# Mixture-of-experts kernel: rows stored in token order, gathered by the experts, instead of scattered by the router

## The chip, the cores and the metric

One core of one Trainium2 chip runs the whole program. The metric is device time in microseconds (us), the median of the runs. Engines: TensorE (PE; its weight loads are PEld), VectorE (DVE), ScalarE (ACT), GpSimd (POOL) and SyncE (SP), whose queue issues most transfers.

## What is computed

x has 4 x 1024 tokens of 256 values. Two layers follow each other, each a cross attention and a feed-forward block. The change lies in the last block, a mixture of 8 experts with 2 of them for each token. Cut to what matters:

```python
logits = layernorm(x) @ Wr + br                  # 4096 x 8
top2 values and indices -> weights w (softmax over the two)
for each token t, for each of its two experts e:
    h = relu(layernorm(x)[t] @ W1[e] + b1[e])    # 256 -> 1024
    out[t] += w * (h @ W2[e] + b2[e])            # 1024 -> 256, on top of the residual x[t]
```

## The kernel before

The 32 tiles of 128 tokens pass through two stages, `route` and `experts`, each a block of its own: all engines leave a block together, and the next one's work begins after that.

**route.** ScalarE normalises a tile into a ring `pay` (`norm`, L1885; 4 buffers of 4 tiles), TensorE transposes it and multiplies it by Wr, ScalarE copies the transposed tile (`copy`, L1891). Every four tiles make a chunk: VectorE picks the two experts of each token (`choose`), ScalarE takes the exponential (`ratio`, L1900), and VectorE (`place`) writes expert, weights and token number beside the row and computes, from a running count per expert (TensorE products with a triangle and with ones, `rank`), the place of each row in a table sorted by expert, `xs` in HBM. GpSimd then scatters each tile's rows twice, once for each expert, with indirect DMAs (L1828, 64 of them, 130 KB each). `norm` waits until the scatters that used its buffer have landed. Between these, 16 halves of W2 come through a ring of four (`load_half`, L1781, SP's queue), ScalarE makes their f16 high part (`high`, L1895) and VectorE their low part (`low`, L1971); the halves of a chunk are split after `place` of that chunk, and half q is loaded once half q-4 is split. The list HIGHS puts two halves into each of chunks 1 to 5 and three into chunks 6 and 7. At the end VectorE computes which expert each of the 32 whole tiles (256 rows) and of the 7 half tiles (128 rows) belongs to, and SP writes rows of padding behind each expert's last row.

**experts.** 36 tiles: 32 of 256 rows with one expert each, then 4 "mixed" ones made of the 7 half tiles. Each engine runs its own list of steps k; in step k

- TensorE turns tile k+2 (`turn_x`, L2184, waits for its rows), multiplies tile k+1 by W1 (`up`) and tile k by W2 (`down`), in this order;
- ScalarE makes the high part of the turned tile k+2 (`high_x`), then the relu of tile k+1;
- VectorE takes the low part of the turned tile k+2 (`rest_x`, L2279), then weighs the result of tile k-1 (`weigh`: yb L2300, yo L2308), then handles the token numbers and splits the relu's output (L2288, L2290);
- GpSimd adds the weighed rows of a tile into the output in HBM, 128 rows at a time, with an accumulating indirect DMA (`add`, L2333), each only after the one before it has landed;
- SP loads the rows of tile k+3 (260 KB, plain DMA, two buffers) once its buffer is free.

A step's signals are semaphores that count tiles; an engine's instructions run in the order of its list.

Of the kernel before, what the change touches and what calls it, by code (L numbers as in the profile page):

```python
# [19 lines left out]
F32 = mybir.dt.float32  # L20
# [1690 lines left out]
def route(nc, w, router, b1T, eid, x_res, mv, rstd, nmr, ident, w2, ssq, sums, unscale, xs, acc, table):  # L1711
# [3 lines left out]
    NB = 4  # L1715
    NK = NT // TK
    NS = 4
    HIGHS = ((),) + 5 * ((1, 3),) + 2 * ((0, 1, 3),)
    with Scope(nc, "rt") as s:
# [16 lines left out]
        posf = s.sb("posf", [P, TK, 2])  # L1736
        pos = [s.sb(f"pos{j}", [P, TK, 2], U32) for j in range(NB)]
        tok = s.sb("tok", [P, NT], U32)
        base = s.sb("base", [P, E])
# [6 lines left out]
        ntf, nti, jump = s.sb("ntf", [P, 2, E]), s.sb("nti", [P, 2, E], I32), s.sb("jump", [P, 2, E])  # L1746
        cum, want, give, left = (s.sb(n, [P, 2, E]) for n in ("cum", "want", "give", "left"))
        whole, lone, spare, twice = s.sb("whole", [P, E + 1]), s.sb("lone", [P, E]), s.sb("spare", [P, 1]), s.sb("twice", [P, 1])
        tid = s.sb("tid", [P, ND + NH])
        ge = s.sb("ge", [P, ND + NH, E])  # L1750
        tf = s.sb("tf", [P, 2, ND + NH])
# [4 lines left out]
        (cst, xn_r, t_r, xt_r, sc_mm, sc_r, c, e_r, d_r, b1_t, b1_c, ind_r, rank_mm, cnt_r, padded,  # L1756
         meta_r) = (s.sem(n) for n in (
            "cst", "xn_r", "t_r", "xt_r", "sc_mm", "sc_r", "c", "e_r", "d_r", "b1_t", "b1_c", "ind_r",
            "rank_mm", "cnt_r", "padded", "meta_r"))
        sent = [s.sem(f"sent{j}") for j in range(NB * TK)]  # L1760
# [14 lines left out]
        @block.sync  # L1775
        def _(sp):
            def load_half(q):
                src = w["L1_ffn_W2"]
                rows = src.shape[1] // 2
                need(sp, wlo_r, q - NS + 1)  # L1780
                sp.dma_start(stage[q % NS][:, :].rearrange("p (t n) -> p t n", n=src.shape[2]),  # L1781
                             src[q // 2, (q % 2) * rows:(q % 2 + 1) * rows, :].rearrange("(t p) n -> p t n", p=P)
                             ).then_inc(half_in[q % NS], 16)

            for q in range(NS):
                load_half(q)
            router["copy"](sp, E - 1)
            for q in range(NS, 2 * E):
                load_half(q)
            sp.wait_ge(cst, CONSTS)  # L1790
            for q in range(TR // P):
                sp.dma_start(xs[E * CAP + q * P:E * CAP + (q + 1) * P, :], pad[:, :]).then_inc(padded, 16)
            sp.wait_ge(cnt_r, 1)
            for e in range(E):
                n = nc.sync.value_load(cnt[0:1, e:e + 1], min_val=0, max_val=T)
                for q in range(TR // P):
                    sp.dma_start(xs[bass.ds(n + (e * CAP + q * P), P), :], pad[:, :]).then_inc(padded, 16)
            sp.wait_ge(padded, 16 * (E + 1) * (TR // P))
            sp.wait_ge(acc_in, 16 * E)

        @block.gpsimd
        def _(pool):
# [3 lines left out]
            g.iota(base[:, :], pattern=[[CAP, E]], base=0, channel_multiplier=0,  # L1806
# [5 lines left out]
            g.memset(whole[:, E:E + 1], 0.0).then_inc(cst, 1)  # L1812
# [5 lines left out]
            pool.wait_ge(cst, 10)  # L1818
            g.affine_select(out=tri[:, :], in_=tri[:, :], compare_op=ALU.is_gt, fill=0.0, base=0,
                            pattern=[[1, P]], channel_multiplier=-1).then_inc(cst, 1)  # L1820
            g.memset(run[:, :], 0.0).then_inc(cst, 1)

            last_row = g.to_reg(E * CAP - 1)
            for t in range(NT):
                c, i = divmod(t, TK)
                pool.wait_ge(meta_r, c + 1)
                for k in range(2):
                    g.indirect_dma_start(out=xs[:, :], out_offset=bass.IndirectOffsetOnAxis(ap=pos[c % NB][:, i, k:k + 1], axis=0),  # L1828
                                         in_=pay[c % NB][:, i, :], in_offset=None, bounds_check=last_row,
                                         oob_is_err=True).then_inc(sent[t % (NB * TK)], 16)  # L1830
            for j in range(NB * TK):
                pool.wait_ge(sent[j], 32 * len(range(j, NT, NB * TK)))

        @block.tensor
        def _(pe):
# [21 lines left out]
            def rank(c):  # L1857
                pe.wait_ge(ind_r, c + 1)
                if c == 0:
                    pe.wait_ge(b1_c, 1)  # L1860
                    pe.wait_ge(bmr_r, 1)
                nc.tensor.matmul(ps_c[0][:, 0:TK * E], tri[:, :], ind[:, :, :], start=True, stop=True).then_inc(rank_mm, 1)
                nc.tensor.matmul(ps_c[1][:, 0:TK * E], ones[:, :], ind[:, :, :], start=True, stop=True).then_inc(rank_mm, 1)

            for t in range(NT):
# [7 lines left out]
                if t % TK == 2 and t > TK:  # L1873
                    rank(t // TK - 1)
            score(NT - 1)
            rank(NK - 1)

        @block.scalar
        def _(act):
            def norm(t):  # L1880
                c, i = divmod(t, TK)
                need(act, sent[t % (NB * TK)], 32 * (c // NB))
# [14 lines left out]

            def ratio(c):
                act.wait_ge(d_r, c + 1)
                nc.scalar.activation(wt[:, 1, :], wt[:, 0, :], ACT.Exp).then_inc(e_r, 1)  # L1900
# [4 lines left out]
            for t in range(NT):  # L1905
# [10 lines left out]
            ratio(NK - 1)  # L1916

        @block.vector
        def _(dve):
# [62 lines left out]
            def choose(c):  # L1982
# [11 lines left out]
                link_on(last)  # L1994
                link_on(v.tensor_copy(idf[:, :, :], idx[:, :, 0:2]))
                if c == 0:
                    dve.wait_ge(cst, CONSTS)
                for n in range(2):
                    last = v.tensor_tensor(oh[:, n, :, :], idf[:, :, n].unsqueeze(2).to_broadcast([P, TK, E]),
                                           eid[:, :].unsqueeze(1).to_broadcast([P, TK, E]), ALU.is_equal)  # L2000
                link_on(last)
                v.tensor_tensor(ind[:, :, :], oh[:, 0, :, :], oh[:, 1, :, :], ALU.add).then_inc(ind_r, 1)

            def place(c):

                out = pay[c % NB]
                for i in range(TK):
                    need(dve, sent[c % NB * TK + i], 32 * (c // NB))
# [3 lines left out]
                link_on(v.tensor_tensor(out[:, :, D + 2], wt[:, 1, :], wt[:, 2, :], ALU.mult))  # L2012
                v.tensor_tensor(out[:, :, D + 1], wt[:, 2, :], out[:, :, D + 2], ALU.subtract)
                v.tensor_copy(out[:, :, D], idf[:, :, 0])
                v.tensor_copy(out[:, :, D + 3].bitcast(U32), tok[:, TK * c:TK * c + TK])

                dve.wait_ge(rank_mm, 2 * (c + 1))
                link_on(v.tensor_copy(tot[:, :, :], ps_c[1][:, 0:TK * E].rearrange("p (t e) -> p t e", e=E)))
                for e in range(E):
                    last = v.tensor_tensor_scan(incl[:, :, e], ones[:, 0:TK], tot[:, :, e], run[:, e:e + 1],  # L2020
                                                ALU.mult, ALU.add)
                link_on(last)
                v.tensor_copy(run[:, :], incl[:, TK - 1, :])

                link_on(v.tensor_tensor(tot[:, :, :], incl[:, :, :], tot[:, :, :], ALU.subtract))
                link_on(v.tensor_tensor(tot[:, :, :], ps_c[0][:, 0:TK * E].rearrange("p (t e) -> p t e", e=E), tot[:, :, :],
                                        ALU.add))
                link_on(v.tensor_tensor(tot[:, :, :], tot[:, :, :], base[:, :].unsqueeze(1).to_broadcast([P, TK, E]), ALU.add))
                for n in range(2):
                    last = v.tensor_tensor(oh[:, n, :, :], oh[:, n, :, :], tot[:, :, :], ALU.mult)  # L2030
                link_on(last)
                for n in range(2):
                    last = v.tensor_reduce(posf[:, :, n], oh[:, n, :, :], AX.X, ALU.add)
                link_on(last)
                v.tensor_copy(pos[c % NB][:, :, :], posf[:, :, :]).then_inc(meta_r, 1)
# [13 lines left out]
            then(v.tensor_copy(cnt[:, :], run[:, :]))  # L2049
            dve.sem_inc(cnt_r, 1)  # L2050

            def per_tile(x, k):
                return x.unsqueeze(1).to_broadcast([P, (ND, NH)[k], E])
# [15 lines left out]
            v.tensor_tensor(whole[:, 0:E], ntf[:, 0, :], lone[:, :], ALU.add)  # L2069
            then(v.scalar_tensor_tensor(out=left[:, 0, :], in0=left[:, 0, :], scalar=2.0, in1=left[:, 1, :],  # L2070
                                        op0=ALU.mult, op1=ALU.add))
            v.tensor_tensor_scan(cum[:, 0, :], ones[:, 0:E], whole[:, 0:E], 0.0, ALU.mult, ALU.add)
            v.tensor_scalar(jump[:, 0, :], whole[:, 0:E], -1.0, float(CAP // TR), ALU.mult, ALU.add)
            v.tensor_tensor(lone[:, :], whole[:, 1:E + 1], whole[:, 0:E], ALU.subtract)
            v.tensor_scalar(twice[:, :], whole[:, 0:1], 2.0, None, ALU.mult)
# [376 lines left out]
```

## Time and profile before

| | us |
|---|---|
| median of 3 runs (1394.09 to 1397.82) | 1396.09 |
| the profiled execution | 1395.44 |
| its span in the profile | 1393.7 |
| all before the routing stage (0 to 856) | 856 |
| routing stage up to the last scores (856 to 941) | 85 |
| from there to the first transpose of the experts (941 to 969) | 28 |
| expert stage (969 to the end) | 425 |

The profile's times count from the start of the span. A row of a timeline gives start, duration, engine, line, operation, output<-input, shape, count, and in brackets how long the engine had been idle before it and what ended that. "PEclk" is the granted share of TensorE's clock (1.00 is 2.4 GHz, 0.50 is 1.2 GHz). "Landing" is the time from a transfer's issue until its semaphore says that it is done.

### The profile page before, as it was taken

The numbers are of one execution on the slowest core, as the hardware profiler recorded it, in microseconds if no ns is written. First come the engines' busy times: TensorE is split into PE (matmuls) and PEld (weight loads), VectorE is DVE, ScalarE is ACT, GpSimd is POOL, SyncE is SP. The second block draws the span as 40 slices with busy tenths as digits, with TensorE's granted clock in tenths as the row PEclk, the third lists the DMA queues.
The fourth block names the chain that finished last, engine by engine and source line by source line (L and its number), as shares of the span: only waits on it lengthen the run. The fifth ranks groups of instructions, "written<-read, shape, count | busy, mean of one in ns | idle before, by whom it ended". The sixth has DMA issues, their size and how long they took to land. (4 is left out here: it accounts for less than half of the span.)

```text
span 1393.7 us, 28305 instructions
## 1 busy us (share of the span) xinstructions
PE 1207.5 (87%) x8633; PEld 922.0 (66%) x8634; DVE 1023.8 (73%) x2058; ACT 802.4 (58%) x1214; POOL 519.4 (37%) x423
## 2 busy tenths in 40 slices
PE   8799999959987767998999997631999999999995
PEld 4457777734432555785777776621889898999874
DVE  5879999887999594786989897944565666656542
ACT  4675656466599697557888886630434344333341
POOL 2077777600000001004888882773123222232222
PEclk9899999989999557999999998555999999999998
DMA  6010000000034873002234323564222323322210
GB/s 232 9 64 1 0 0 0 0 1 0 23 159 178 263 260 131 1 1 66 77 93 125 99 91 125 184 201 153 43 48 46 49 46 47 53 46 45 48 30 7
DMA packets 61448, 106.07 MB, mean 76 GB/s; under 512 B 7488, under 2 KB 48704, under 8 KB 60736
## 3 DMA queue, kind: packets, MB, share of 16 engines
q1 hardware_dynamic: 48080, 88.24, 19.9%
q0 software_dynamic: 13296, 16.92, 6.5%
q8 instruction: 38, 0.62, 0.2%
q14 instruction: 34, 0.28, 0.1%
HBM read 66.96 MB, written 39.10 MB: 76 GB/s over the span
## 5 line engine op out<-in xcount | busy, mean ns | idle before, releaser
L2333 POOL DMA_INDIRECT out<-ex_yo,ex_mt x71 | 114.2, 1608 | 317.2 <-DVE ex_yo L2308 169.0
L2242 ACT ACTIVATE ex_hT<-ex_ps_h,e_b1T,e_unscale 128x256 f32<-128x256 f32 (+1 forms) x312 | 143.9, 545 | 114.5 <-PE ex_ps_h L2199 114.5
L2199 PE MATMUL ex_ps_h<-ex_xT_hi,a_arena 128*128 128x256 f16 (+1 forms) x1248 | 202.7, 266 | 0.6 <-issue 0.5
L604 PE MATMUL at_ps_y<-c_VW,at_pT_hi 128*128 (+1 forms) x1024 | 171.1, 273 | 3.5 <-DVE main_x_res L752 3.5
L946 POOL TENSOR_TENSOR at_sc<-at_sc,at_ri 128x960 f32<-128x960 f32 (+1 forms) x96 | 144.9, 1523 | 56.4 <-DVE at_ri L747 56.0
L2199 PE MATMUL ex_ps_h<-ex_xT_lo,a_arena 128*128 128x256 f16 (+1 forms) x624 | 164.1, 264 | 0.0
L946 POOL TENSOR_TENSOR at_sc<-at_sc,at_mx 128x960 f32<-128x960 f32 (+1 forms) x96 | 134.1, 1411 | 70.3 <-DVE at_mx L724 70.2
L2212 PE MATMUL ex_ps_y<-a_arena,ex_hT_hi 128*128 x568 | 155.7, 274 | 4.8 <-DVE ex_hT_lo L2290 2.7
L582 PE MATMUL at_ps_s<-a_arena,at_xnT_hi 128*128 (+1 forms) x512 | 155.1, 385 | 3.0 <-issue 2.9
L2212 PE MATMUL ex_ps_y<-e_w_lo,ex_hT_hi 128*128 x568 | 155.7, 274 | 0.0
L2212 PE MATMUL ex_ps_y<-a_arena,ex_hT_lo 128*128 x568 | 155.6, 274 | 0.0
L1189 PE MATMUL gm_bank<-f_xq,f_wide 128*128 (+1 forms) x576 | 129.3, 385 | 13.3 <-DVE f_xq L1281 7.0
L604 PE MATMUL at_ps_y<-c_VW,at_pT_lo 128*128 (+1 forms) x512 | 139.6, 273 | 0.0
L2199 PEld LDWEIGHTS ex_ps_h<-ex_xT_hi,a_arena 128*128 x1248 | 121.6, 98 | 18.2 <-issue 1.9
L643 ACT COPY at_sc<-at_ps_s 128x1024 f32<-128x1024 f32 x64 | 64.7, 1010 | 98.5 <-PE at_ps_s L582 98.5
L1189 PEld LDWEIGHTS gm_bank<-f_xq,f_wide 128*128 128x128 f16 x576 | 55.9, 99 | 86.5 <-issue 8.9
L604 PEld LDWEIGHTS at_ps_y<-c_VW,at_pT_hi 128*128 128x128 f16 x1024 | 100.0, 98 | 15.0 <-issue 4.2
L2233 ACT ACTIVATE ex_xT_hi<-ex_ps_t 128x512 f16<-128x512 f32 (+1 forms) x36 | 21.3, 591 | 150.5 <-PE ex_ps_t L2184 150.5
L724 DVE TENSOR_REDUCE at_mx<-at_sc 128x16 f32<-128x960 f32 (+1 forms) x96 | 79.0, 850 | 38.6 <-ACT at_sc L643 38.6
L582 PE MATMUL at_ps_s<-a_arena,at_xnT_lo 128*128 (+1 forms) x256 | 98.2, 384 | 0.0
L2288 DVE CAST ex_hT_hi<-ex_hT 128x1024 f16<-128x1024 f32 (+1 forms) x72 | 52.6, 731 | 56.9 <-ACT ex_hT L2242 56.8
L2279 DVE SCALAR_TENSOR_TENSOR ex_xT_lo<-ex_ps_t,ex_xT_hi 128x512 f16<-128x512 f32 (+1 forms) x36 | 24.6, 684 | 91.1 <-ACT ex_xT_hi L2233 91.1
(352 smaller groups left out, 2778.7 us busy)
## 6 DMA issues: line engine op xcount, KB each, us to landing
at_half<-in_L_ffn_W SPq DMA_DIRECT2D x32, 512.0 KB, 4.1
up_scratch<-gm_stg SPq DMA_DIRECT2D x16, 768.0 KB, 3.2
gm_stg<-up_scratch SPq DMA_DIRECT2D x16, 768.0 KB, 4.3
ex_row<-xs SPq DMA_DIRECT2D x32, 260.0 KB, 3.0
rt_stage<-in_L_ffn_W SPq DMA_DIRECT2D x16, 512.0 KB, 4.8
main_x_res<-in_x SPq DMA_DIRECT2D x8, 512.0 KB, 12.0
out<-main_x_res SPq DMA_DIRECT2D x8, 512.0 KB, 6.4
xs<-rt_pad SPq DMA_DIRECT2D x18, 130.0 KB, 2.4
```

Source lines behind the costliest of these rows:

```text
L582: last = nc.tensor.matmul(ps_s[j][:, c * CH:(c + 1) * CH], a[:, d, :], b[:, d, bass.ds(off + c * CH, CH)], start=(n == 0), stop=(n == 3 * ...
L604: last = nc.tensor.matmul(ps_y[:, 0:D], a[j][:, n, :], b[:, bass.ds(off + n * D, D)], start=(n == 0 and i == 0), stop=(n == NP - 1 and i = ...
L643: nc.scalar.copy(sc[j][:, :, :], ps_s[j % 2][:, :].rearrange("p (h k) -> p h k", h=H)).then_inc(ev_r, 1)
L724: last = nc.vector.tensor_reduce(mx[:, j, :, g], sc[j][:, :, lo:hi], AX.X, ALU.max)
L946: last = nc.gpsimd.tensor_tensor(part, part, what[:, j, :, g].unsqueeze(2).to_broadcast([P, H, hi - lo]), op)
L1189: last = nc.tensor.matmul(ps[:, o, :], a[:, d, o * P:(o + 1) * P], b[:, d, bass.ds(c0, CH)], start=(n == 0), stop=(n == 3 * DT - 1))
L2199: last = nc.tensor.matmul(ps_h[:, n, at], a[:, bass.ds(e * WN + d * HID + n * P, P)], b[:, d, at], start=(m == 0), stop=(m == 3 * DT - 1))
L2212: last = nc.tensor.matmul(ps_y[j][:, q, :], a[:, n, q * P:(q + 1) * P], b[:, bass.ds(e * WN + n * D, D)], start=(n == 0 and m == 0), stop= ...
L2242: last = nc.scalar.activation(hT[:, n, at], ps_h[:, n, at], ACT.Relu, bias=b1T[:, bass.ds(e * HT + n, 1)], scale=unscale[:, 0, bass.ds(e, 1)])
L2279: nc.vector.scalar_tensor_tensor(out=xT_lo[j][:, :, at], in0=ps_t[:, :, at], scalar=XN_SCALE, in1=xT_hi[j][:, :, at], op0=ALU.mult, op1=AL ...
L2288: nc.vector.tensor_copy(hT_hi[j][:, part, at], hT[:, part, at]).then_inc(hhi_r, 1)
L2333: nc.gpsimd.indirect_dma_start(out=acc[:, :], out_offset=bass.IndirectOffsetOnAxis(ap=mt[j][:, q, 1:2].bitcast(U32), axis=0), in_=yo[j][:, ...
```

## The change

- Each normalised row is written once, in token order, with plain DMAs from ScalarE's queue (`send`, one per chunk of 4 tiles, 520 KB), two chunks after its normalisation; the ring `pay` has three buffers instead of four. The 64 scatters and SP's 16 writes of padding behind the experts' rows go; one block of padding rows is written.
- The small sums and copies beside the rows move from VectorE to GpSimd; the ranks of all tiles are computed at once after the last chunk, by two larger products.
- A list `slot` is made in their place: for each of the 71 blocks of 128 rows and each lane, the number of the row in `xs`. VectorE writes 0/1 masks (`spread`, four groups of 16 token columns: 71 x 16, 71 x 16 and 128 x 16 values per partition), ScalarE scales one of them, and 64 products on TensorE add them up.
- In the expert stage GpSimd fetches a block's rows with an indirect DMA through `slot` (two for each tile, four row buffers); SP loads nothing but b2. Of a whole tile both additions are issued without waiting for one another; they wait for those of the tile before. The loops are unrolled by four tiles instead of two.

The core of the diff (renamed indices, sizes and semaphores left out):

```diff
 # route, ScalarE
+            def send(c):
+                act.wait_ge(xn_r, TK * (c + 1))
+                act.wait_ge(pay_r, c + 1)
+                nc.scalar.dma_start(xs[(TK * c + 1) * P:(TK * (c + 1) + 1) * P, :].rearrange("(i p) d -> p i d", p=P),
+                                    pay[c % NB][:, :, :]).then_inc(sent[c % NB], 16)
...
-                need(act, sent[t % (NB * TK)], 32 * (c // NB))
+                need(act, sent[c % NB], 16 * (c // NB))
...
                 if t % TK == 1 and t > TK:
                     ratio(t // TK - 1)
+                if t % TK == 1 and t > 2 * TK:
+                    send(t // TK - 2)
                 if i in HIGHS[c]:
                     high(highs_to(c) + HIGHS[c].index(i))
             ratio(NK - 1)
+            send(NK - 2)
+            send(NK - 1)
+            for g in range(NG):
+                act.wait_ge(spot_r, g + 1)
+                need(act, slot_mm, g - 1)
+                nc.scalar.activation(in_slot[g % 2][:, 1, :, :], is_slot[g % 2], ACT.Copy, scale=lane[:, 0:1]).then_inc(slot_r, 1)
 # route, VectorE, place(c): all but the first two operations go (weights and token numbers to GpSimd)
                 link_on(v.tensor_scalar(wt[:, 0, :], wt[:, 1, :], 1.0, None, ALU.add))
-                link_on(v.reciprocal(wt[:, 2, :], wt[:, 0, :]))
...
+                v.reciprocal(wt[:, 2, :], wt[:, 0, :]).then_inc(inv_r, 1)
 # route, VectorE, after the last chunk (some 20 small operations between, the quotas as before)
+            dve.wait_ge(rank_mm, 1)
+            dve.wait_ge(xn_r, NT)
+            dve.wait_ge(acc_in, 16 * E)
+            then(v.tensor_copy(tot[:, :, :], ps_c[1][:, 0:NT * E].rearrange("p (t e) -> p t e", e=E)))
+            for e in range(E):
+                last = v.tensor_tensor_scan(incl[:, :, e], ones[:, 0:NT], tot[:, :, e], 0.0, ALU.mult, ALU.add)
...
+            def spread(g):
+                mine, t0 = slice(GR * g, GR * g + GR), GR * g % NT
+                need(dve, slot_r, g - 1)
+                need(dve, turn_r, g - 1)
+                v.tensor_tensor(is_slot[g % 2], line[:, 0:SLOTS].unsqueeze(1).to_broadcast([P, GR, SLOTS]),
+                                part_f[:, 1, mine].unsqueeze(2).to_broadcast([P, GR, SLOTS]), ALU.is_equal).then_inc(spot_r, 1)
+                need(dve, slot_mm, g - 1)
+                dve.wait_ge(spot_r, g + 1)
+                v.tensor_tensor(in_slot[g % 2][:, 0, :, :], is_slot[g % 2],
+                                turn_no[:, t0:t0 + GR].unsqueeze(2).to_broadcast([P, GR, SLOTS]), ALU.mult).then_inc(turn_r, 1)
+                v.tensor_tensor(in_lane[:, mine, :], line[:, :].unsqueeze(1).to_broadcast([P, GR, P]),
+                                part_f[:, 0, mine].unsqueeze(2).to_broadcast([P, GR, P]), ALU.is_equal).then_inc(lane_r, 1)
...
             lows(highs_to(NK - 1), highs_to(NK))
+            dve.wait_ge(slot_mm, NG)
+            then(v.tensor_copy(lane_v[:, :], ps_i[:, SLOTS:2 * SLOTS]))
+            v.scalar_tensor_tensor(out=slot[:, :], in0=ps_i[:, 0:SLOTS], scalar=float(P), in1=lane_v[:, :], op0=ALU.mult, op1=ALU.add)
 # experts, GpSimd (RB = 4, Q = 2; SP's load() goes)
+            def fetch(i, q):
+                need(pool, t_r, i - RB + 1)
+                need(pool, meta_r, i - RB + 1)
+                n = 2 * i + q
+                nc.gpsimd.indirect_dma_start(out=row[i % RB][:, q, :], out_offset=None, in_=xs[:, :],
+                                             in_offset=bass.IndirectOffsetOnAxis(ap=slot[:, n:n + 1].bitcast(U32), axis=0),
+                                             bounds_check=last_sent, oob_is_err=True).then_inc(row_in[i % RB], 16)
+            def add(i, q):
                 pool.wait_ge(yo_r, i + 1)
-                for q in range(rows_of(i).stop):
-                    need(pool, added, 16 * (Q * i + q))
+                need(pool, added, 16 * (Q * i + (q if mixed(i) else 0)))
                 pool.sem_inc(begun, 1)
...
+            for i in range(RB):
+                for q in range(Q):
+                    fetch(i, q)
+            for k in range(1, NTL + 1):
+                for q in range(rows_of(k - 1).stop):
+                    add(k - 1, q)
+                if there(k + 3, NTL):
+                    for q in range(rows_of(k + 3).stop):
+                        fetch(k + 3, q)
```

## Rows read from the trace of the kernel before

**Rows 1.** Stretches of the span: busy time of each engine, clock, DMA.
```profile
core 0: us, PE busy (x) PEld busy (x) DVE busy (x) ACT busy (x) POOL busy (x), PEclk, DMA share, GB/s
...
820.00:856.00 36.00, 28.89 (x235) 23.25 (x233) 30.51 (x70) 23.74 (x36) 21.14 (x23) 1.00 0.24 74
...
880.00:890.00 10.00, 6.09 (x28) 5.77 (x28) 9.14 (x59) 5.85 (x12) 7.87 (x8) 0.50 0.66 217
...
1060.00:1100.00 40.00, 40.00 (x369) 35.99 (x367) 25.49 (x43) 17.24 (x35) 11.11 (x7) 1.00 0.31 50
```

**Rows 2.** Timeline of GpSimd in the routing stage, the scatters.
```profile
868.85 1.33 POOL L1828 DMA_INDIRECT xs<-rt_pay,rt_pos  x1 [11.36 <-DVE rt_pos L2035]
...
885.84 1.86 POOL L1828 DMA_INDIRECT xs<-rt_pay,rt_pos  x1 [0.30 <-issue]
...
956.39 0.97 POOL L1828 DMA_INDIRECT xs<-rt_pay,rt_pos  x1 [0.30 <-issue]
```

**Rows 3.** Timeline of ScalarE in the routing stage.
```profile
869.66 0.37 ACT L1891 COPY rt_xt<-rt_ps_t 128x256 f32<-128x256 f32 x1
...
891.16 1.15 ACT L1895 ACTIVATE a_arena<-rt_stage,rt_wsc 128x1024 f16<-128x1024 f32 x1 [2.17 <-DMA rt_stage<-in_L_ffn_W]
...
896.27 0.37 ACT L1891 COPY rt_xt<-rt_ps_t 128x256 f32<-128x256 f32 x1
...
936.44 1.15 ACT L1895 ACTIVATE a_arena<-rt_stage,rt_wsc 128x1024 f16<-128x1024 f32 x1 [10.43 <-DMA rt_stage<-in_L_ffn_W]
```

**Rows 4.** One line, L1781: the halves of W2, issue to landing.
```profile
DMA to landing us min/median/max: 4.2/4.8/7.1
```

**Rows 5.** One line, L1828: the scatters, issue to landing.
```profile
DMA to landing us min/median/max: 2.4/3.1/7.2
```

**Rows 6.** One line, L2333: the additions, issue to landing.
```profile
DMA to landing us min/median/max: 2.7/4.0/6.2
```

**Rows 7.** Timeline, from the last scores to the first expert matmul.
```profile
940.37 0.19 DVE L1985 TENSOR_TENSOR rt_scores<-rt_ps_r,e_brb 128x32 f32<-128x32 f32 x1 [5.80 <-PE rt_ps_r L1853]
...
942.31 0.19 DVE L2002 TENSOR_TENSOR rt_ind<-rt_oh 128x32 f32<-128x32 f32 x1
...
946.87 0.17 DVE L2055 TENSOR_SCALAR rt_nti<-rt_cnt 128x8 int32<-128x8 int32 x1
...
949.79 0.17 DVE L2077 SCALAR_TENSOR_TENSOR rt_jump<-rt_lone,rt_left 128x8 f32<-128x8 f32 x1
...
952.69 3.68 DVE L1971 SCALAR_TENSOR_TENSOR e_w_lo<-rt_stage,rt_wsc,a_arena 128x1024 f16<-128x1024 f32 x3
...
973.30 0.39 PE L2199 MATMUL ex_ps_h<-ex_xT_hi,a_arena 128*128 128x256 f16 x1
```

**Rows 8.** Groups by line and shape, VectorE, routing and expert stages.
```profile
L2020 DVE TENSOR_TENSOR_SCAN rt_incl<-rt_ones,rt_run,rt_tot 128x4 f32<-128x4 f32 x64 | 9.4, 220 | 0.3
...
L2086 DVE TENSOR_TENSOR rt_ge<-rt_ge,rt_jump 128x256 f32<-128x256 f32 x1 | 0.4, 426 | 0.0
...
L2290 DVE TENSOR_TENSOR ex_hT_lo<-ex_hT,ex_hT_hi 128x1024 f16<-128x1024 f32 x70 | 85.8, 1225 | 2.4
```

**Rows 9.** Timeline of the expert stage: transposes of a tile, products, additions.
```profile
991.42 0.60 PE L2184 MATMUL ex_ps_t<-main_ident,ex_row 128*128 128x128 f32 x4
...
1089.67 0.60 PE L2184 MATMUL ex_ps_t<-main_ident,ex_row 128*128 128x128 f32 x4
...
1092.91 0.69 DVE L2308 TENSOR_TENSOR ex_yo<-ex_yb,ex_mt 128x512 f32<-128x512 f32 x1
...
1094.48 1.62 POOL L2333 DMA_INDIRECT out<-ex_yo,ex_mt  x1 [3.96 <-DVE ex_yo L2308]
...
1100.17 1.54 POOL L2333 DMA_INDIRECT out<-ex_yo,ex_mt  x1 [4.07 <-DMA out<-ex_yo,ex_mt]
...
1319.47 0.60 PE L2184 MATMUL ex_ps_t<-main_ident,ex_row 128*128 128x128 f32 x4
...
1333.95 0.60 PE L2184 MATMUL ex_ps_t<-main_ident,ex_row 128*128 128x128 f32 x4
```

More of the change, by code:

```diff
@@ L56 @@
 NTL = ND + NM
+SLOTS = 2 * ND + NH
 EPS = 1e-5
@@ L2014, in place @@
[L2014 to L2030, printed above, removed]
@@ new lines, in _ @@
+            then(v.tensor_tensor(begin[:, 1, :], begin[:, 1, :], begin[:, 0, :], ALU.subtract))
+            then(v.tensor_tensor(incl[:, :, :], incl[:, :, :], begin[:, 1, :].unsqueeze(1).to_broadcast([P, NT, E]), ALU.mult))
+            then(v.tensor_tensor(after[:, :, :], after[:, :, :], incl[:, :, :], ALU.add))
+            for i in range(2):
+                last = v.tensor_tensor(oh[:, i, :, :], oh[:, i, :, :], after[:, :, :], ALU.mult)
+            then(last)
+            then(v.tensor_reduce(spot[:, :], oh[:, :, :, :].rearrange("p n t e -> p (n t) e"), AX.X, ALU.add))
@@ L2099, in experts @@
+            lows(highs_to(NK - 1), highs_to(NK))
+            dve.wait_ge(slot_mm, NG)
+            then(v.tensor_copy(lane_v[:, :], ps_i[:, SLOTS:2 * SLOTS]))
+            v.scalar_tensor_tensor(out=slot[:, :], in0=ps_i[:, 0:SLOTS], scalar=float(P), in1=lane_v[:, :],
+                                   op0=ALU.mult, op1=ALU.add)
+def experts(nc, b2, b1T, eid, x_res, w1, w2, unscale, ident, xs, acc, table, slot):
     Q = TR // P
     with Scope(nc, "ex") as s:
-        row = [s.sb(f"row{j}", [P, Q, ROW]) for j in range(2)]
+        RB = 4
+        row = [x_res[:, E:, :].rearrange("p t d -> p (t d)")[:, j * Q * ROW:(j + 1) * Q * ROW].rearrange("p (q d) -> p q d", q=Q)
+               for j in range(RB)]
@@ L2144, in landed, with in_fours @@
             if not mixed(i):
[L2145 to L2148 removed]
+                return 16 * Q * (i // RB + 1)
+            return 16 * (Q * ND // RB + sum(len(runs(m)) for m in range(ND + i % RB, i + 1, RB)))
+        def in_fours(eng, lead, lag, step):
             for k in range(-lead, 4):
[L2151 to L2156 removed]
+                step(k, k % RB)
+            with eng.Fori(1, ND // RB - 1, 1) as i:
+                for j in range(RB):
+                    step(RB * i + j, j)
+            for k in range(ND - RB, NTL + lag):
+                step(k, k % RB)
         @block.sync
         def _(sp):
[L2160 to L2173 removed]
             sp.dma_start(b2s, b2.unsqueeze(0).to_broadcast([P, E, D])).then_inc(b2_in, 16)
[L2175 removed]
         @block.tensor
@@ L2187, in up @@
             def up(i, j):
-                spans = [(look_up(nc.tensor, 1, n, E - 1), slice(q0 * P, q1 * P)) for n, q0, q1 in runs(i)]
+                spans = [(expert(nc.tensor, n), slice(q0 * P, q1 * P)) for n, q0, q1 in runs(i)]
                 pe.wait_ge(xhi_r, i + 1)
@@ L2204, in down @@
             def down(i, j):
-                spans = [(look_up(nc.tensor, 1, n, E - 1), range(q0, q1)) for n, q0, q1 in runs(i)]
+                spans = [(expert(nc.tensor, n), range(q0, q1)) for n, q0, q1 in runs(i)]
                 pe.wait_ge(hlo_r, 2 * i + 2)
@@ L2235, in relu @@
             def relu(i, j):
-                spans = [(look_up(nc.scalar, 1, n, E - 1), slice(q0 * P, q1 * P)) for n, q0, q1 in runs(i)]
+                spans = [(expert(nc.scalar, n), slice(q0 * P, q1 * P)) for n, q0, q1 in runs(i)]
                 for g in range(2):
@@ L2259, in take_meta @@
                 q = rows_of(i)
-                nc.vector.tensor_copy(meta[j][:, q, :], row[j][:, q, D:ROW]).then_inc(meta_r, 1)
+                nc.vector.tensor_copy(meta[j % 2][:, q, :], row[j][:, q, D:ROW]).then_inc(meta_r, 1)
             def keep_meta(i, j):
-                spans = [(look_up(nc.vector, 1, n, E - 1), slice(q0, q1)) for n, q0, q1 in runs(i)]
+                spans = [(expert(nc.vector, n), slice(q0, q1)) for n, q0, q1 in runs(i)]
                 need(dve, added, 16 * Q * (i - 1))
@@ L2293, in weigh @@
             def weigh(i, j):
-                spans = [(look_up(nc.vector, 1, n, E - 1), slice(q0, q1)) for n, q0, q1 in runs(i)]
+                spans = [(expert(nc.vector, n), slice(q0, q1)) for n, q0, q1 in runs(i)]
                 if isinstance(i, int) and i == 0:
```

255 lines of the change are left out of this document (125 added, 130 removed).

## The prediction

> **What bounds the kernel now.** I read the busy time of the engines by stretches first, then the timeline of each stage that the change touches, then single lines for the landing times.
>
> In the expert stage TensorE is the bound: between 1060 and 1100 it is busy 40.00 of 40 us at full clock [rows 1]. The transposes that open its steps (I call that time X) stand at 991.42 for the turn of tile 3 and at 1319.47 for tile 33, 30 steps of 10.93 us [rows 9]. GpSimd's waits there are long, for the weighed rows and for the addition before, but TensorE waits for none of them.
>
> In the routing stage TensorE does not count (6.09 of 10 us, clock 0.50, which is 1.2 GHz [rows 1]). GpSimd sends 64 scatters from 868.85 on, the last starting at 956.39, one each 1.27 us (0.97 and a gap of 0.30) with few breaks [rows 2]; VectorE waits for them before it may write beside a row. ScalarE waits for halves of W2 that SP can load only after VectorE's split, 10.43 us the longest [rows 3]. So this stage is a chain of scatters and VectorE's chunks, and its end a tail of 32.9 us from the last scores (940.37) to the first expert product (973.30) [rows 7].
>
> **The change, part 1: the routing stage up to the last scores.** The scatters go; with them the pace of 10 us per chunk. What is late next is ScalarE. Without a wait it does two highs and four pairs of norm and copy from 891.16 to 896.64, 5.48 us, so 1.05 for a high and 0.85 for a pair [rows 3]. But with three buffers the norm of the first tile of chunk C+1 waits for the send of chunk C-2, which ScalarE issued only one high and one pair earlier. No row shows a send from this queue. The nearest is a half of W2, about the same size: 4.2 to 7.1 us, median 4.8 [rows 4]; I take 4.8. After the wait come three pairs, a high and the exponential, 3.8 us: 8.6 us a chunk. The first such send can go after the copy that ended at 870.03 [rows 3], so at 870.2; four chunks later 904.6, with the third high of chunk 6 905.7. Then two waits for halves of W2 remain that the change doesn't remove: the half is loaded after `place` and one split (1.9 us), and lands 4.8 us later, 6.7 in all. The first takes us to 912.4, two highs, two pairs and the exponential to 916.4, the second to 923.1. In the kernel before, the high after this same wait started at 936.44 and the last scores were there at 940.37 [rows 3, 7], 3.9 later. So now 927.0 in place of 940.4: 13.4 us earlier. With 4.2 in all six waits it is 17.0, with 7.1 nothing (0.4 later).
>
> The sends' issue on ScalarE I cost inside the 4.8, behind which nothing else waits. The sums moved to GpSimd are hidden: it has nothing else to do in this stage, and `send` of a chunk comes two chunks later; without that cover each would cost ScalarE about 1 us a chunk. The rank products per chunk leave TensorE, which isn't the bound: nothing.
>
> **Part 2: the tail.** From the last scores, all on one chain: `choose` up to the masks 1.9 (940.37 to 942.3 [rows 7]); GpSimd's sum and the first rank product 1.7 (estimate: before, two products of an eighth of the columns and VectorE's sum took 1.4); copy, 8 scans of 32 and differences 3.2 (0.22 for a scan of 4 and 0.43 for 256 elements [rows 8]; a scan between 0.15 and 0.5, I take 0.25); the quotas as before 2.9 (946.87 to 949.79 [rows 7]); twelve operations for the positions 5.1 (five of 256 at 0.43, one of 512, the rest at 0.2 [rows 7, 8]); the masks: 256 elements take 0.43 and 1024 take 1.225 us, so 1.04 ns an element [rows 8], 1.3 for 1136 and 2.3 for 2048, four groups of 4.9, 19.5; the table of tiles 1.3; three lows 3.7 [rows 7]; the list itself 0.5. That makes 39.8. ScalarE's scaling and TensorE's 64 products run under the masks and the lows; without that cover they would add some 4 us. Then leaving the block 0.3, four fetches issued in 5.1 (0.97 and a gap of 0.30, as the scatters [rows 2]), landing 3.1 [rows 5], transposes 1.1: 49.4 in place of 32.9. The tail is 16.5 us longer (13.5 to 19.5 with the scans, the small operations and the landing at their ends). What went from it, the last scatters and the writes of padding, is contained in the 32.9.
>
> Both parts: 16.5 - 13.4 = 3.1 us later, from 3.5 earlier to 20 later.
>
> **Part 3: the expert stage.** "Four tiles ahead" counts buffers. On GpSimd, whose list is in order, the fetch of tile k+3 stands behind the two additions of tile k-1. Their rows are ready only in step k, because VectorE's `weigh` of k-1 stands behind `rest_x` of k+2, which needs the transposes that open step k. And the transposes of tile k+3 open step k+1. So the rows are asked for in one step and needed at the start of the next, and the way round is a loop: transposes, low part, weigh, two additions, two fetches, landing, next transposes. Its length from the rows: transposes at 1089.67, weighed rows at 93.60, first addition issued at 94.48 [rows 9], 4.81 after X. It keeps GpSimd 1.62. The second follows at once now (before, at 1100.17); the gap is between 0.30, as from scatter to scatter [rows 2], and 0.88, as from the weighed rows to the first addition; with a semaphore between I take 0.6. Second addition 1.54 [rows 9], then gap 0.30, fetch 0.97, gap 0.30, fetch 0.97; no row shows a fetch, the nearest is a scatter of the same rows [rows 2]. The last is issued at X + 11.1, already later than X + 10.93, where TensorE wants the tile. Landing 3.1 [rows 5]: next X at 14.2 in place of 10.93, 3.27 us of stall. TensorE, which turns first in its step, holds `up` and `down` behind it. It happens for the turns of tiles 4 to 33, 30 steps: 98 us. The two steps after 1319.47 take 14.5 and more even now (1319.47 to 1333.95 [rows 9]), so nothing is added there.
>
> Bounds: gap 0.30 and landing 2.4 give 13.2, 68 us; gap 0.88, second addition 1.62 and one fetch at the 1.86 of a disturbed scatter [rows 2] give 15.5, 137 us. A gain is excluded, since a stage at 40.00 of 40 can't go faster by transfers.
>
> The Trainium skill speaks against this part (SBUF — State Buffer, "Who interferes with whom"): a VectorE cast in its two-port mode and GpSimd's writing of descriptors shut each other out. In each step VectorE has two such casts of 0.7 us; by the rule a step would be about 14.9 long, and the whole 1518.
>
> The additions side by side are worth nothing by themselves: they end a wait of GpSimd's that TensorE doesn't feel. Two whole steps of unrolling more: no row shows a loop's cost, and with TensorE at 40.00 of 40 across the loops of before there is none to save. SP's loads that go were hidden under TensorE. The end of the kernel (half tiles, whose additions still wait for one another) stays as it is.
>
> **Sum.** 1395.44, the profiled execution, + 3.1 + 98 = 1497 (it lies 0.65 under the median of the runs, inside their spread).
>
> **Rivals.**
>
> *The fetch is hidden (not slower).* If GpSimd were free at once after each of its four instructions, so that from the first addition to landing there were less than 10.93 - 4.81 = 6.1 us, no step would stall, and only the routing parts count: 1398, between 1392 and 1415. For it: GpSimd's spans are rough. Against it: 64 scatters in 87.5 us [rows 2] show that each does cost 1.27, and 4 x 1.27 alone leave 1.0 us for a landing that took 2.4 at the least [rows 5]. Chance 0.04, half of it within 0.3%, a quarter faster. Between this and my bounds, with landing nearer 2 us and short instructions, 1415 to 1455: 0.05.
>
> *The fetch waits for both additions to land.* Then it comes only 4.0 us (up to 6.2 [rows 6]) after the second addition at X + 8.6, and lands 3.1 later: steps of 15.7 to 17.9, 1541 to 1607. For it: they are of the same queue. Against: nothing in the program makes one wait for the other. Chance 0.07. The Trainium skill (DMA: Bandwidth & Descriptors, "SWDGE vs HWDGE vs iDMA") has one single queue for all that GpSimd issues; no row here shows whether a later transfer is held up by it.
>
> *The stalls take the clock down.* With 3 us idle in 14, TensorE at 1.2 GHz would need 21.9 us a step: 1728. For it: 0.50 at 6.09 busy of 10 in the routing stage. Against: between 820 and 856 it was busy 28.89 of 36, about the share that I forecast (10.9 of 14.2), at 1.00 [rows 1]. Chance 0.02.
>
> **Numbers.** The forecast, a loop of 13.2 to 15.5 us, has 0.82. The range goes from 1455 to 1555: 1395.4 + 68 - 3.5 at the lower end (1460, and a little into the case between), 1395.4 + 137 + 20 at the upper. A difference under 0.3% (4 us) is what a measurement can't tell from no change. Faster by more 0.02, within it 0.03, slower 0.95.
>
> **What would show it.** Steps of some 14 us in place of 10.93 between transposes; idle time of TensorE before the transposes, ended by the fetch, about 30 times 3 us; GpSimd with two additions and two fetches close together in each step; last scores near 927; about 49 us from there to the first expert product. Were the steps 10.9 long, part 3 is wrong; if fetches start only when additions have landed, or take GpSimd far more or less than 1 us each, its size is.

## The result, and the profile after

The changed kernel takes 1475.94 us (median of three, 1473.56 to 1476.85) against 1396.09: 1.0576 times as long, 95% interval 1.0560 to 1.0591. The profiled execution has a span of 1474.2, against 1393.7 before. The forecast was 1497, the range 1455 to 1555. Further down, medians leave out executions over 1.5% above the fastest of their kernel; three profiled ones (one fetch ahead, the split subtraction, the first run with half-precision masks) are of a kind that reaches the routing stage some 19 us later (873.9 to 876.8 in place of 855.8 to 857.6), and only what lies behind that point is read from them.

Set beside each other at the transposes X, the two spans part into three. Tile 3 is turned at 982.44 in place of 991.42 [rows 9]: the routing stage and the first tiles are 8.98 us shorter. From there to the turn of tile 33 at 1397.26 there are 30 steps of 13.83 in place of 10.93: 86.8 longer. From there to the end it is 76.9 in place of 74.2, 2.7 longer. Together 80.5.

**The expert stage.** Busy time by stretches: two steps and all 30 (columns as in [rows 1]):

```profile
core 0: us, PE busy (x) PEld busy (x) DVE busy (x) ACT busy (x) POOL busy (x), PEclk, DMA share, GB/s
...
1038.79:1052.68 13.89, 12.81 (x101) 10.52 (x101) 6.69 (x11) 4.46 (x9) 6.39 (x4) 0.88 0.24 39
...
1052.68:1066.44 13.76, 11.31 (x101) 9.72 (x101) 6.64 (x11) 4.46 (x9) 6.30 (x4) 1.00 0.25 41
...
982.44:1397.26 414.82, 357.65 (x3003) 301.14 (x3001) 198.96 (x330) 133.69 (x270) 187.72 (x120) 0.95 0.24 38
```

TensorE, busy without a break before, is busy 357.65 of 414.82 us. Its clock is down to 0.88 to 0.90 in 12 of the 30 steps. Of the two steps shown the one with the slow clock, 12.81 of 13.89 busy, is hardly longer than the other, 11.31 of 13.76: its matmuls fill what would have been idle. So not TensorE sets the step. What it waits for there, all 30 steps (waits of TensorE):

```profile
engine line waited for: us in total, times, longest us
...
PE ex_ps_t L2219 <- DMA main_x_res<-xs,e_slot: 46.3, 30, 3.2
...
PE ex_ps_h L2234 <- issue: 10.8, 28, 0.5
```

The fetched rows end 46.3 of the 57.2 us of idle time; the rest is 28 gaps of at most 0.5 behind the transposes.

One step from transposes to transposes (timelines of PE, VectorE and GpSimd, merged):

```profile
1148.19 0.66 PE L2219 MATMUL ex_ps_t<-main_ident,main_x_res 128*128 128x128 f32 x4 [0.64 <-DMA main_x_res<-xs,e_slot]
...
1151.28 0.69 DVE L2343 TENSOR_TENSOR ex_yo<-ex_yb,ex_mt 128x512 f32<-128x512 f32 x1
...
1152.85 1.62 POOL L2377 DMA_INDIRECT out<-ex_yo,ex_mt  x1 [6.55 <-DVE ex_yo L2343]
...
1154.77 1.66 POOL L2377 DMA_INDIRECT out<-ex_yo,ex_mt  x1 [0.31 <-issue]
...
1156.73 1.10 POOL L2369 DMA_INDIRECT main_x_res<-xs,e_slot  x1 [0.30 <-issue]
...
1156.89 0.69 DVE L2323 CAST ex_hT_hi<-ex_hT 128x1024 f16<-128x1024 f32 x1 [0.64 <-ACT ex_hT L2277]
...
1157.62 1.23 DVE L2325 TENSOR_TENSOR ex_hT_lo<-ex_hT,ex_hT_hi 128x1024 f16<-128x1024 f32 x1
...
1158.13 1.64 POOL L2369 DMA_INDIRECT main_x_res<-xs,e_slot  x1 [0.30 <-issue]
...
1161.61 0.66 PE L2219 MATMUL ex_ps_t<-main_ident,main_x_res 128*128 128x128 f32 x4 [1.68 <-DMA main_x_res<-xs,e_slot]
```

This is the loop, from X = 1148.19: first addition at X + 4.66, 1.62 long, gap 0.30, second 1.66, 0.30, fetch 1.10, 0.30, fetch 1.64, and 1.84 from its end to the next transposes: 13.42. The next thing to see is the second fetch. It starts inside the subtraction L2325 (1157.62 to 1158.85) and ends 0.92 after its end. In each of the 30 steps just one of the two fetches starts inside such a subtraction; these 30 all end 0.92 to 0.98 after it and take 1.54 to 1.85, the other 30 take 1.05 to 1.24. A fetch that has started before is not held up: the one at 1156.73 runs across the whole cast L2323, and into the subtraction, in 1.10. A fetch that starts early in a cast does not occur here (it does in the run with the subtraction in halves).

**The routing stage.** ScalarE's timeline (ACTq: the issue of a send), and VectorE's first work on the last scores:

```profile
869.96 0.40 ACTq L1926 DMA_DIRECT2D xs<-rt_pay  x1
...
873.41 0.60 ACT L1910 ACTIVATE rt_pay<-main_x_res,main_nmr,main_rstd 128x256 f32<-128x256 f32 x1 [1.10 <-DMA xs<-rt_pay]
...
896.64 0.37 ACTq L1926 DMA_DIRECT2D xs<-rt_pay  x1
...
903.66 1.15 ACT L1920 ACTIVATE a_arena<-rt_stage,rt_wsc 128x1024 f16<-128x1024 f32 x1 [2.34 <-DMA rt_stage<-in_L_ffn_W]
...
913.18 1.15 ACT L1920 ACTIVATE a_arena<-rt_stage,rt_wsc 128x1024 f16<-128x1024 f32 x1 [5.72 <-DMA rt_stage<-in_L_ffn_W]
...
917.11 0.19 DVE L2025 TENSOR_TENSOR rt_scores<-rt_ps_r,e_brb 128x32 f32<-128x32 f32 x1 [5.59 <-PE rt_ps_r L1869]
```

The sends follow each other every 6.7 us (869.96 to 896.64, four chunks). `norm` waits for a send five times, 0.70 to 1.18, 4.8 in all. The two waits for halves of W2 that the prediction expected are there, 2.34 and 5.72. The last scores come at 917.11, 23.3 earlier than in [rows 7].

**The tail** (timeline):

```profile
930.52 1.34 DVE L2120 TENSOR_TENSOR main_x_res<-rt_line,rt_part_f 128x1136 f16<-128x1136 f32 x1
...
935.49 2.07 PE L1886 MATMUL rt_ps_i<-main_x_res 128*128 128x142 f16 x16 [14.04 <-DVE main_x_res L2126]
...
947.78 2.28 DVE L2126 TENSOR_TENSOR main_x_res<-rt_line,rt_part_f 128x2048 f16<-128x2048 f32 x1
...
951.17 3.67 DVE L2011 SCALAR_TENSOR_TENSOR e_w_lo<-rt_stage,rt_wsc,a_arena 128x1024 f16<-128x1024 f32 x3
...
955.01 0.23 DVE L2140 SCALAR_TENSOR_TENSOR e_slot<-rt_ps_i,rt_lane_v 128x71 int32<-128x71 f32 x1
...
956.46 1.38 POOL L2369 DMA_INDIRECT main_x_res<-xs,e_slot  x1 [36.44 <-SPq L81]
...
961.05 1.12 PE L2219 MATMUL ex_ps_t<-main_ident,main_x_res 128*128 128x128 f32 x4 [8.86 <-DMA main_x_res<-xs,e_slot]
...
964.76 0.39 PE L2234 MATMUL ex_ps_h<-ex_xT_hi,a_arena 128*128 128x256 f16 x1
```

From the last scores to the masks 13.4, masks 19.5, remainders of W2 3.67, the list at 955.24, first fetch 956.46, first expert product 964.76: 47.65 in place of 32.9.

### The profile page after: what moved, and what is told of

It is laid out like the page before. It is cut to its first block and busy times, and to the rows that moved or that the text cites. A ratio compares the mean times of both kernels' runs of the same rounds, so it can differ in the third digit from the quotient of the medians.

```text
span 1474.2 us, 27795 instructions
## 1 busy us (share of the span) xinstructions
PE 1242.2 (84%) x8669; PEld 931.0 (63%) x8670; DVE 1019.6 (69%) x1906; ACT 807.2 (55%) x1218; POOL 575.5 (39%) x470
## 5 line engine op out<-in xcount | busy, mean ns | idle before, releaser
L2234 PE MATMUL ex_ps_h<-ex_xT_hi,a_arena 128*128 128x256 f16 (+1 forms) x1248 | 220.7, 279 | 11.9 <-issue 10.8
L2377 POOL DMA_INDIRECT out<-ex_yo,ex_mt x71 | 120.8, 1701 | 272.0 <-DVE ex_yo L2343 245.2
L2234 PE MATMUL ex_ps_h<-ex_xT_lo,a_arena 128*128 128x256 f16 (+1 forms) x624 | 172.7, 278 | 0.0
L2234 PEld LDWEIGHTS ex_ps_h<-ex_xT_hi,a_arena 128*128 x1248 | 127.7, 103 | 42.9 <-issue 20.1
L2323 DVE CAST ex_hT_hi<-ex_hT 128x1024 f16<-128x1024 f32 (+1 forms) x72 | 52.1, 724 | 98.5 <-ACT ex_hT L2277 98.2
L2369 POOL DMA_INDIRECT main_x_res<-xs,e_slot x71 | 97.2, 1369 | 57.8 <-SPq L81 36.4
```

The lines of the kernel that those rows point to most:

```text
L2234: last = nc.tensor.matmul(ps_h[:, n, at], a[:, bass.ds(e * WN + d * HID + n * P, P)], b[:, d, at], start=(m == 0), stop=(m == 3 * DT - 1))
L2323: nc.vector.tensor_copy(hT_hi[j][:, part, at], hT[:, part, at]).then_inc(hhi_r, 1)
L2369: nc.gpsimd.indirect_dma_start(out=row[i % RB][:, q, :], out_offset=None, in_=xs[:, :], in_offset=bass.IndirectOffsetOnAxis(ap=slot[:, n:n ...
L2377: nc.gpsimd.indirect_dma_start(out=acc[:, :], out_offset=bass.IndirectOffsetOnAxis(ap=mt[i % 2][:, q, 1:2].bitcast(U32), axis=0), in_=yo[i ...
```

## Experiments

Each run had its own runs of the kernel before on the same chip beside it, medians 1394.7 to 1395.7.

**Fetches first.**

```diff
 for k in range(1, NTL + 1):
+    if there(k + 3, NTL): fetch(k + 3, q) for each q
     add(k - 1, q) for each q
-    if there(k + 3, NTL): fetch(k + 3, q) for each q
```

> GpSimd issues the two fetches of tile k+3 ahead of the two additions of tile k-1; nothing else differs from the changed kernel. Theory (the loop from transposes over additions and fetches back to transposes sets the step): the loop is open, the fetches land a step early, steps fall from 13.83 to 10.9 us, TensorE's 46 us of waits for fetches go, and the time is 1476 - 30 x 2.9 = 1389 (1384 to 1394), some 7 under the kernel before, since its routing stage ends 8 us earlier. Rival (four software instructions a step, or one queue for fetches and additions, slow the stage wherever they stand): steps of 12 or more, 1425 or more.

Measured: 1389.64 (median of six, 1388.04 to 1407.49), ratio 0.9991 (0.9942 to 1.0039): against the kernel before, the gain of 6 us is not clear of the noise, against the changed kernel the 86 us are. All 30 steps are 10.92 us. The expert stage of this run by stretches (columns as above):

```profile
990.00:1300.00 310.00, 310.00 (x2842) 279.15 (x2841) 193.29 (x311) 126.04 (x255) 199.69 (x114) 1.00 0.30 48
```

and its GpSimd in one step (timeline):

```profile
1064.41 1.69 POOL L2377 DMA_INDIRECT out<-ex_yo,ex_mt  x1 [3.17 <-DVE ex_yo L2343]
...
1066.40 2.40 POOL L2377 DMA_INDIRECT out<-ex_yo,ex_mt  x1 [0.31 <-issue]
...
1069.11 1.85 POOL L2369 DMA_INDIRECT main_x_res<-xs,e_slot  x1 [0.30 <-issue]
...
1071.26 1.05 POOL L2369 DMA_INDIRECT main_x_res<-xs,e_slot  x1 [0.30 <-PE ex_ps_t L2219]
```

GpSimd does the same four instructions, and they even take longer (the second addition 2.40, the first fetch 1.85: in all 30 steps both start during a subtraction of VectorE), but TensorE is busy 310.00 of 310 us at full clock. So neither GpSimd's load nor a common queue makes the step, only the place of the fetches in the list. The rival is out. The prediction's case in which a fetch waits for the additions to land is not decided by this run, in which a fetch has a whole step to spare; it is by the trace of the changed kernel (see the rivals below).

**A tile's additions one after the other again**, in the changed kernel: `need(pool, added, 16 * (Q * i + q))` in `add`.

> The changed kernel with a tile's second addition waiting for the landing of its first again. Theory (loop): the second addition starts some 5.7 us after the first, as before, in place of 1.93, and this enters each of 30 steps whole: steps of 17.6, time 1476 + 30 x 3.8 = 1590 (1570 to 1610). Rival (side by side is worth nothing, since the second addition's rows move only when the first's have landed, or since TensorE does not feel GpSimd's waits): 1476 to 1485.

Measured: 1567.25, ratio 1.1232 (1.1199 to 1.1265); 30 steps of 16.80. GpSimd, one step (timeline):

```profile
1153.10 1.62 POOL L2377 DMA_INDIRECT out<-ex_yo,ex_mt  x1 [6.51 <-DVE ex_yo L2343]
...
1157.73 1.98 POOL L2377 DMA_INDIRECT out<-ex_yo,ex_mt  x1 [3.02 <-issue]
...
1160.02 1.85 POOL L2369 DMA_INDIRECT main_x_res<-xs,e_slot  x1 [0.30 <-issue]
...
1162.17 1.05 POOL L2369 DMA_INDIRECT main_x_res<-xs,e_slot  x1 [0.30 <-issue]
```

Here the second addition starts 4.63 after the first, in the step of the changed kernel shown above 1.92; the means of 30 steps are 4.89 and 1.94, not 5.7 as I had it from the kernel before, so the time lies under the range. The step is 2.97 longer, nearly all of it this 2.95, and 30 of them are 89 of the 91 us. So additions side by side are worth 3 us a step where they stand in the loop.

**The same with the fetches first:**

> Fetches first, and a tile's second addition waiting for the first again. Theory: out of the loop, additions side by side are worth nothing: same time as with fetches first alone, within 4 us (1389). Rival (additions side by side relieve GpSimd's list or the queue also outside the loop): 5 us or more slower than with fetches first alone.

Measured: 1387.96, ratio 0.9952 (0.9938 to 0.9965), 1.7 from the run with fetches first alone, steps 10.92. Outside the loop they are worth nothing.

**One fetch ahead of the additions, one behind.**

> One of a tile's two fetches goes ahead of the additions, the other stays behind them. Theory (loop): the loop loses one fetch and one gap, 1.1 to 1.6 + 0.3: steps of 12.0 to 12.5, time 1420 to 1436. Rival (the fetches behind the additions wait for the additions' transfers in the queue, so that the way to the landing is not the sum of issue times): the remaining fetch lands as late as now, steps 13.5 to 13.9, 1465 to 1478.

Measured: 1426.3, ratio 1.022 (1.020 to 1.024). In the profile the 30 steps are 12.00 on average, most of them 11.5 to 11.7. One instruction taken from the chain is worth what it takes there, and the fetch left behind the additions does not wait for them: the one at 1157.32 starts 0.30 after the second addition's issue and lands 3.0 after its start.

**The subtraction in halves**, in the changed kernel:

```diff
-nc.vector.tensor_tensor(hT_lo[j][:, part, at], hT[...], hT_hi[j][...], ALU.subtract)
+for half in (first two of the four, last two):
+    nc.vector.tensor_tensor(hT_lo[j][:, half, at], hT[...], hT_hi[j][...], ALU.subtract)
```

> The changed kernel, with VectorE's subtraction for the low part of the hidden rows (1.23 us, twice a step) cut into two halves each. Theory (a fetch whose issue falls into this subtraction starts only at its end, which is why fetches take 1.1 or 1.85 us): a fetch waits for half as long at most, some 0.35 us a step, 30 steps: 1476 - 11 = 1465 (1460 to 1470). Rival (the length of a fetch's issue has nothing to do with this subtraction, or the second half catches it again): 1474 to 1478.

Measured: 1457.0, ratio 1.0434 (1.0415 to 1.0454), 18.9 less than the changed kernel, nearly twice what the theory gave and under its range; 30 steps of 13.16. GpSimd's groups between 990 and 1400, of the changed kernel:

```profile
L2377 POOL DMA_INDIRECT out<-ex_yo,ex_mt x59 | 101.3, 1718 | 201.6 <-DVE ex_yo L2343 185.1 <-issue 16.5
...
L2369 POOL DMA_INDIRECT main_x_res<-xs,e_slot x60 | 84.7, 1411 | 18.3 <-issue 18.3
```

and with the subtraction in halves:

```profile
L2379 POOL DMA_INDIRECT out<-ex_yo,ex_mt x60 | 99.6, 1659 | 222.1 <-DVE ex_yo L2345 205.5 <-issue 16.6
...
L2371 POOL DMA_INDIRECT main_x_res<-xs,e_slot x60 | 68.3, 1138 | 18.3 <-issue 18.3
```

The mean fetch falls from 1.41 to 1.14: nearly all of the delay is gone, not half. Two fetches and two additions are 0.66 a step shorter, 20 us in 30 steps. That the subtraction holds back the fetch is borne out. Why more than half of the delay goes is seen in the timeline (VectorE and GpSimd merged; first a usual step, then the longest fetch of the 30 steps):

```profile
1142.30 0.69 DVE L2326 TENSOR_TENSOR ex_hT_lo<-ex_hT,ex_hT_hi 128x512 f16<-128x512 f32 x1
...
1142.83 1.09 POOL L2371 DMA_INDIRECT main_x_res<-xs,e_slot  x1 [0.31 <-issue]
...
1314.87 0.69 DVE L2323 CAST ex_hT_hi<-ex_hT 128x1024 f16<-128x1024 f32 x1 [0.57 <-ACT ex_hT L2277]
...
1314.98 1.51 POOL L2371 DMA_INDIRECT main_x_res<-xs,e_slot  x1 [0.30 <-issue]
```

In all 30 steps one of the two fetches starts inside the first half and still ends 0.92 to 0.98 after that half; but it starts only 0.10 to 0.49 before the half's end (median 0.17), and the second half, which starts after the fetch, does not hold it. The cast does the same as the subtraction: the fetch at 1314.98 starts 0.58 before the end of a cast and ends 0.93 after it, and one at 1393.38 likewise.

**Remainders of W2 early**, with fetches first:

```diff
+lows(halves of chunk m cast before its last tile)
 choose(m)
+lows(the half cast at its last tile)
 place(m)
-if m < NK - 1: lows(highs_to(m), highs_to(m + 1))
 ...
-lows(highs_to(NK - 1), highs_to(NK))        # in the tail
```

> Fetches first, and each remainder of a half of W2 split off as soon as ScalarE has written its high part, ahead of the weights of the two experts; none is left for the tail. Theory (the two waits for halves of W2, 2.3 and 5.7 us in the changed kernel, come from splits that stand behind the chunk's weights; the tail is VectorE's list): these waits go, -8, less some 1.5 of new waits for sends, and the tail loses 2.3 (three remainders of 3.67, under which 2.07 us of products were hidden): 1389 - 9 = 1380 (1377 to 1384). Rival (the sends' landing is what paces ScalarE, as the prediction had it): waits for sends take the place of the waits for halves whole and only the tail's 2.3 are left: 1386 to 1390.

Measured: 1380.5, ratio 0.991 (0.9885 to 0.9936), 9.1 under fetches first alone. ScalarE's waits from 850 to 925:

```profile
ACT rt_pay L1910 <- DMA xs<-rt_pay: 5.7, 5, 2.5
...
ACT a_arena L1920 <- DMA rt_stage<-in_L_ffn_W: 0.7, 1, 0.7
```

The halves now cost 0.7 in place of 8.1, and the waits for sends stay what they were (5.7 against 4.8). Last scores at 911.02, first transposes at 953.51. Counted from the first `norm` of the stage, the last scores come 7.8 earlier than with fetches first alone, and the way from there to the first transposes is 1.4 shorter, where I had 2.3. So the sends were not what stood behind the long waits. Whether a fourth buffer would take away the waits for sends was not tried.

**Masks in half precision**, on top of that: all operands f16, laid out with the 16 columns of a group innermost, so that the products read columns with a stride of 16 elements.

> As the run with early remainders, and the masks of the list made with all operands in half precision and in the layout in which none is repeated along the innermost direction (a constant pattern written by GpSimd, products read with a stride). Theory (VectorE's 19.5 us of masks set the tail, by their elements and the layout): operations at about half their time, tail 9.6 shorter, 1371 (1368 to 1375). Rival (the masks keep their time, or the 64 products read with a stride set the pace instead): 1378 to 1382.

Measured: 1377.6, ratio 0.9875 (0.9861 to 0.9889). VectorE's first masks, TensorE's products and the list (timeline):

```profile
946.44 0.75 DVE L2131 TENSOR_TENSOR main_x_res<-main_x_res,rt_part_f 128x1136 f16<-128x1136 f16 x1
...
947.89 1.22 DVE L2137 TENSOR_TENSOR main_x_res<-main_x_res,rt_part_f 128x2048 f16<-128x2048 f16 x1
...
949.17 17.06 PE L1894 MATMUL rt_ps_i<-main_x_res 128*128 128x142 f16 x64 [11.78 <-DVE main_x_res L2137]
...
966.53 0.23 DVE L2150 SCALAR_TENSOR_TENSOR e_slot<-rt_ps_i,rt_lane_v 128x71 int32<-128x71 f32 x1
```

1136 elements take 0.75 in place of 1.34, 2048 take 1.22 in place of 2.28. The Trainium skill (VectorE: DVE Perf Modes, "What auto-detection actually checks") makes 16-bit operands with steps of one the condition for VectorE's mode `2×_1P`; the run agrees, though type and layout were changed together and it does not show what each does alone. But the 64 products take 17.06, 0.27 each, where 16 took 2.07 in the changed kernel (935.49), 0.13 each, both at a granted clock of 0.50. The list stands 20.3 after the first mask, against 22.2: the rival's mechanism came true, with a time just under its range.

**The same in pairs**, with a stride of two.

> As the run with half-precision masks, but laid out in pairs: two columns of the list stand side by side, so that no operand is repeated along the innermost direction and the products read with a stride of two elements in place of sixteen. Theory (the stride of sixteen doubled the products' time; a stride of two does not): masks 10.9 us, products of 2.07 us a group again under them, the list some 13.5 us after the masks' start in place of 22.2 with early remainders alone: 1380 - 8.7 = 1372 (1369 to 1375). Rival (any stride costs the same, 64 products of 0.27 = 17 us set the pace): 1377 to 1380, as with the stride of sixteen.

Measured: 1373.9, ratio 0.9832 (0.979 to 0.988), 21 under the kernel before beside it. In the tail (timeline: the first mask, the products of the first and of the last group, the list):

```profile
929.77 0.75 DVE L2125 TENSOR_TENSOR main_x_res<-rt_line,rt_part_f 128x1136 f16<-128x1136 f16 x1
...
932.50 2.08 PE L1886 MATMUL rt_ps_i<-main_x_res 128*128 128x142 f16 x16 [11.78 <-DVE main_x_res L2131]
...
940.38 1.25 PE L1886 MATMUL rt_ps_i<-main_x_res 128*128 128x142 f16 x16 [1.40 <-DVE main_x_res L2131]
...
941.93 0.23 DVE L2144 SCALAR_TENSOR_TENSOR e_slot<-rt_ps_i,rt_lane_v 128x71 int32<-128x71 f32 x1
```

List 12.4 after the first mask. The first 16 products take 2.08 at a granted clock of 0.50, as without a stride; the last 16 take 1.25, as the clock has come back to 1.00. Of the 9.8 won in the tail 6.5 are seen in the time; in this execution the last scores were some 4 later than with early remainders alone, with one wait of `norm` for a send of 3.00. What lengthens such a wait stays open.

## Why the prediction was right

**The loop (part 3) was right, its sum by luck closer than its terms.** Forecast 14.2 a step and 98 us, measured 13.83 and 86.8. That it is a loop through GpSimd's list is shown from three sides: ahead of the additions the fetches cost nothing, with one of them ahead less than half of the cost is left, and a longer chain costs 3 us more a step. In the step shown, 4.81 to the first addition was 4.66, the gap taken at 0.6 was 0.30, the second addition 1.66 in place of 1.54. Two terms were wrong in opposite ways. I added the landing of 3.1 [rows 5] to the end of the last fetch's issue. Such landings count from its start, for in the step shown even the next transposes start only 1.84 after its end and 3.48 after its start. So a fetch's 0.97 stood in the sum twice. And I gave each fetch 0.97, while one of the two in each step is held to 1.5 or more. Over the 30 steps the two fetches take 1.44 and 1.38 on average, 0.88 more than forecast, and from the second one's end to the next transposes it is 1.94, 1.16 less. That the additions side by side are worth nothing holds outside the loop only; inside, where my sum had them start one right behind the other, they are worth 3 us a step.

**Part 1 was right in kind and too small**: last scores 23.3 earlier in place of 13.4, past its best case of 17.0. The sends land in 3.4, not 4.8, and the next one goes out 3.3 after the wait and not 3.8, so a chunk takes 6.7 and not 8.6. Over the four chunks (896.64 in place of 904.6) that is 8.0 of the 9.9. The rest lies behind them, where the two waits for halves are 8.1 together in place of 13.4.

**Part 2 was right**: 47.65 against 49.4, the masks 19.5 as worked out from the price of an element. The small operations ahead of them took 13.4 in place of 14.8; leaving the block took 1.2 in place of 0.3, and from the first fetch to the first product it was 8.3 in place of 9.3. Parts 1 and 2 together made the kernel 9 us faster, where I had it 3 slower; the bound was 3.5 faster. This is where the gain of fetches first over the kernel before comes from.

**The end** is 2.7 longer where I had nothing; 1.5 of it is the step after tile 33, 16.02 in place of 14.48, to which the sum added nothing. With the fetches first that step is 14.90, so most of it belongs to the same loop; the rest is open.

**Rivals.** The fetch is not hidden, and it does not wait for the additions to land. In the step shown the first fetch starts at 1156.73, while the second addition lands 3.9 after its start, at 1158.7; and that fetch lands 2.9 after its own start, as do the early ones, issued before any addition (958 to 965: median 2.9).

The clock does fall, to 0.88 to 0.90 in 12 of the 30 steps, and it is 0.88 over the stretch from 1000 to 1400 with additions one after the other. The 12 steps last 14.01 on average, the other 18 13.70. In the two steps shown above the slower clock makes TensorE 1.5 us longer busy; so most of the lost speed is paid out of idle time.

The prediction's price for casts, steps of 14.9, is not there, but the effect is: in the changed kernel no fetch starts more than 0.18 before the end of a cast, and where two do, with the subtraction in halves, they end 0.93 after it. Also, eight casts that start 1.44 to 1.51 after the start of a fetch that is itself held up take 0.82 to 0.89 in place of 0.69. This agrees with the rule of the Trainium skill (SBUF — State Buffer, "Who interferes with whom") that a VectorE cast in its two-port mode and GpSimd's writing of descriptors shut each other out; the mode itself is in no trace. Another sentence of that section, that an instruction of VectorE with two inputs in SBUF gets in the way of a GpSimd instruction that reads SBUF, agrees with the subtraction: it has two such inputs, and a fetch reads its list there.

## What to carry to other kernels

When a transfer is issued by an engine whose list is in order, look at what stands ahead of it in the list and follow it round: if its way leads back to the engine that waits for the transfer, buffers do not help, and each instruction in the loop costs its full length in each step. Count a landing from the point from which the view counts it. And when a stage gets shorter, see which wait was behind the one removed: here two waits for weights, 8.1 us together, of which a reordering on another engine left 0.7. And where an engine that issues transfers takes unevenly long for equal ones, look at what its neighbour was doing when each began.

## What was not expected of the hardware

- A fetch issued by GpSimd that starts during VectorE's subtraction of two tiles in SBUF ends 0.92 to 0.98 us after the subtraction, 30 times of 30 in the changed kernel; one that has started before goes on (1.05 to 1.24). A cast of a tile in SBUF does the same (two fetches, 0.93 after it).
- Not every instruction of VectorE does: with fetches first and additions one after the other, 17 fetches start 0.67 to 0.72 before the end of `yb` (L2335), which reads one of its two tiles from PSUM, and take 1.05 or 1.06.
- The scatter of 1.86 in [rows 2] was a sign of it in the kernel before: it starts 1.01 before the end of a split of W2 (L1971, two tiles in SBUF).
- Products that read both operands with a stride of 16 two-byte elements take 0.27 us each in place of 0.13 at the same clock (0.50); with a stride of two there is no such loss (2.08 for 16).
- A comparison or product of two tiles on VectorE with all operands in half precision, and none repeated along the innermost direction, takes 0.75 us for 1136 elements in place of 1.34.
